# Gate and up products in two passes, the second with seven block products, and the sums of weight blocks on POOL

## Reference

```
x = x + linear_attention(q=layernorm(x), k=ctx, v=ctx)     # softmax of q over 16 dims, of k over tokens; 8 heads
h = layernorm(x)                                           # 2048 tokens x 1024
gate, up = h @ Wg.T, h @ Wu.T                              # Wg, Wu: 2752 x 1024 from codes and scales
x = x + (silu(gate) * up) @ Wd.T                           # Wd: 1024 x 2752
W = NF4[codes] * scales  (one scale per 64 inputs)
```

## Time and profile before

| what | value |
|---|---|
| median of 3 runs | 1540.36 us |
| profiled execution | 1539.45 us, its span 1537.7 us |
| PE busy | 1509.7 us, 98% |
| ACT busy | 921.8 us, 60% |
| DVE busy | 724.2 us, 47% |
| POOL busy | 60.9 us, 4% |
| DMA | 232.93 MB, mean 151 GB/s |

### The profile page before, as it was taken

The page is one execution under the profiler, slowest core; times in us unless marked ns, Lnnn a source line. Parts: engine busy times, 40 slices in busy tenths (PEclk is TensorE's granted clock), DMA queues, the critical chain, the costliest instruction groups (busy, mean ns, idle before and its releaser), DMA issues.

```text
span 1537.7 us, 18265 instructions
## 1 busy us (share of the span) xinstructions
PE 1509.7 (98%) x7056; PEld 1254.1 (82%) x7056; DVE 724.2 (47%) x1106; ACT 921.8 (60%) x1067; POOL 60.9 (4%) x99
## 2 busy tenths in 40 slices
PE   7999999999999999999999999999989999999998
PEld 6888788888888888888888888888768888888787
DVE  6998322322322222322322232222368888888764
ACT  6777876767677767676687767676223333333331
POOL 3343000000000000000000000000000000000000
PEclk9999999999999999999999999999999999999999
DMA  6554434444544454444443444436873535354332
GB/s 214 167 170 135 145 110 149 132 137 130 151 147 134 131 150 133 149 124 143 151 144 120 148 138 129 153 118 227 301 282 124 189 113 192 110 192 151 117 131 82
DMA packets 115462, 232.93 MB, mean 151 GB/s; under 512 B 8240, under 2 KB 55344, under 8 KB 110896
## 3 DMA queue, kind: packets, MB, share of 16 engines
q1 hardware_dynamic: 115376, 231.77, 46.9%
HBM read 154.14 MB, written 77.59 MB: 151 GB/s over the span
## 4 chain that ended last, share of the span: by engine, by line
PE 92%; ACT 4%; DMA 2%; issue 1%; DVE 1%; SPq 0%; DVEq 0%; POOL 0%; ACTq 0%
PE bank L1071 20%; PE bank L1069 20%; PE bank L1070 20%; PE bank L1116 8%; PE bank L1117 8%; PE bank L1118 8%; PE bank L1020 3%; PE bank L1047 1%; PE bank L1054 1%; DMA F<-inter_scratch 1%; PE bank L1037 1%; ACT early L602 1%; DMA inter_scratch<-F 1%; ACT F L615 1%; ACT F L636 1%
## 5 line engine op out<-in xcount | busy, mean ns | idle before, releaser
L1069 PE MATMUL bank<-R 128*128 128x512 f32 x1376 | 535.9, 389 | 0.0
L1070 PE MATMUL bank<-R 128*128 128x512 f32 x1376 | 535.7, 389 | 0.0
L1071 PE MATMUL bank<-R 128*128 128x512 f32 x1376 | 535.7, 389 | 0.0
L581 ACT ACTIVATE F<-F 128x1024 f32<-128x1024 f32 x441 | 467.6, 1060 | 13.3
L1070 PEld LDWEIGHTS bank<-R 128*128 128x128 f32 x1376 | 258.3, 188 | 53.7
L1071 PEld LDWEIGHTS bank<-R 128*128 128x128 f32 x1376 | 258.3, 188 | 53.6
L1069 PEld LDWEIGHTS bank<-R 128*128 128x128 f32 x1376 | 258.4, 188 | 53.3
L717 ACT COPY F<-bank 128x512 f32<-128x512 f32 x120 | 70.5, 587 | 271.0 <-PE bank L1118 267.1
L841 DVE TENSOR_TENSOR F<-F,bank 128x512 f32<-128x512 f32 x84 | 57.6, 686 | 331.1 <-issue 200.0
L648 ACT ACTIVATE F<-bank 128x512 f32<-128x512 f32 x84 | 49.8, 593 | 215.3 <-PE bank L1071 215.2
L767 DVE SCALAR_TENSOR_TENSOR F<-F 128x1024 f32<-128x1024 f32 x63 | 77.2, 1226 | 169.5 <-ACT F L581 169.5
(11 more groups left out here) (92 smaller groups left out, 1479.2 us busy)
## 6 DMA issues: line engine op xcount, KB each, us to landing
wf_scratch<-F SPq DMA_DIRECT2D x70, 512.0 KB, 3.5
inter_scratch<-F SPq DMA_DIRECT2D x84, 256.0 KB, 2.3
F<-in_gu_codes SPq DMA_DIRECT2D x41, 512.0 KB, 5.0
F<-in_gu_scales SPq DMA_DIRECT2D x82, 256.0 KB, 4.2
F<-inter_scratch SPq DMA_DIRECT2D x40, 512.0 KB, 3.8
R<-wf_scratch SPq DMA_DIRECT2D x20, 1024.0 KB, 5.9
FR<-wf_scratch SPq DMA_DIRECT2D x15, 1024.0 KB, 5.9
F<-in_d_codes SPq DMA_DIRECT2D x22, 512.0 KB, 4.4
```

The costliest lines, as they stand in the source:

```text
L581: nc.scalar.activation(y, y, ACT.Prelu, bias=bias, scale=scale, alpha=alpha).then_inc(bent, 1)
L1069: pe.matmul(dst, hi, xh[:, tb, t, :], start=(t == 0), stop=False)
L1070: pe.matmul(dst, hi, xl[:, tb, t, :], start=False, stop=False)
L1071: i = pe.matmul(dst, lo, xh[:, tb, t, :], start=False, stop=(t == HT - 1))
```

## The change

The gate and up stage is split into two passes over the chunks, counted by positions p. `FPOS` = 20 is the position of the half chunk and `FULL` = 21 that of chunk 20.

*Pass 1* does token blocks 0 and 1 as before, two blocks a position (44 entries in `BLOCKS`). In it each weight tile is made from its codes, stored to a new scratch tensor `w_scratch` (512 KB a tile), and split into high and low part by DVE alone (`split`: a copy and a subtraction). The tokens of blocks 2 and 3 are not split: their turned values stay in float32 (`xt`), and during the pass the seven sums and blocks of them are made, two a position, split, and (but for one) stored to `xf_scratch`. They come back as `xform`, each 2 MB.

*Pass 2* does token blocks 2 and 3 together. The matrix of a chunk is cut into gate and up rows and two halves of K, the tokens into two blocks and the same halves; seven products of 12 matmuls each replace eight. For the half chunk four products are enough. For each chunk one load of 1 MB brings gate and up weights back into `staged`, which is one buffer; POOL makes the four sums of its blocks; ACT copies the seven slices (high part) and DVE subtracts (low part). The tiles of Wd and their forms, one tile a position, are made in this pass only; formerly they were made over the whole stage. The buffers are laid out anew, the down stage's `wslot`, `stage`, `aform` and `yacc` with them, and its first loads are issued in another order.

The core of the diff (old lines first):

```diff
-            for c in range(FULL):
-                n = 2 + 3 * c
-                levels_of(act, n, n % 2, loads(n), None if c else last_turns)
-                silu_of(c, 0)
...
+            def weight_sums(p):
+                tt = nc.gpsimd.tensor_tensor
+                pool.wait_ge(staged_in, 16 * (p + 1))
+                wait(pool, wfl_ready, nth(p - 1, NP - 1) if p else 0)
+                wait(pool, ws_ready, p)
+                u = 2 * fulls(p)
+                tt(WS1, A21, A22, ALU.add).then_inc(ws_step, 1)
+                tt(WS3, A11, A21, ALU.subtract)
+                pool.wait_ge(ws_step, u + 1)
+                tt(WS2, WS1, A11, ALU.subtract).then_inc(ws_step, 1)
+                pool.wait_ge(ws_step, u + 2)
+                tt(WS4, A12, WS2, ALU.subtract).then_inc(ws_ready, 1)
+            for p in range(POS):
+                if p != FPOS:
+                    weight_sums(p)
...
...
+            def load_staged(p):
+                c = chunk_of(p)
+                if p:
+                    sp.wait_ge(wfl_ready, nth(p - 1, NP - 1))
...
+            for p in range(POS):
+                if p:
+                    store_pair_out(p - 1, 1)
+                next_item(WN + 2 + p)
+                if p == KW:
+                    store_rest(0)
+                    sp.wait_ge(form_stored, 16 * 2 * NP)
+                    load_w(0, 0)
+                if p + 1 < POS:
+                    load_staged(p + 1)
+                for tb in range(4):
+                    store_form(p, tb)
...
+                store_pair_out(p, 0)
# ACT, pass 1
+            for p in range(FPOS):
+                n = 2 * p + 2
+                if p:
+                    silu_block(2 * p - 1)
+                levels_of(act, n, 0, loads(n), None if p else last_turns)
+                xform_hi(2 * p - 2)
+                silu_block(2 * p)
+                levels_of(act, n + 1, 1, loads(n + 1))
+                xform_hi(2 * p - 1)
...
+            def wform_hi(p, i):
...
+                if p == 0:
+                    act.wait_ge(*((gate_done, 2 * FPOS + 3) if i < 4 else (up_done, ups_until(NB1 - 1))))
+                else:
+                    act.wait_ge(pair_done, nth(p - 1, i))
+                act.wait_ge(ws_ready, p + 1)
...
+                nc.scalar.copy(wslice[i][:, 0], src).then_inc(wfh_ready, 1)
# ACT, a full position of pass 2 (silu_x(p - 1) waits for the last product of p - 1)
+                    silu_x(p - 1)
+                for i in range(4, NP):
+                    wform_hi(p, i)
+                    bend_wd(p, 0, 1)
+                snap1(p)
+                form_hi(p, 0)
+                    bend_wd(p, 1, 2)
+                snapq(p)
+                form_hi(p, 1)
+                    bend_wd(p, 2, 3)
+                snap2(p)
+                bend_wd(p, 3, 4)
+                form_hi(p, 2)
+                wform_hi(p + 1, 0)
+                bend_wd(p, 4, 5)
+                silu_c(p)
+                wform_hi(p + 1, 1)
+                bend_wd(p, 5, 6)
+                wform_hi(p + 1, 2)
+                form_hi(p, 3)
+                bend_wd(p, 6, 7)
+                wform_hi(p + 1, 3)
+                bend_wd(p, 7, 8)
# DVE, a full position of pass 2
+                    pair_out(p - 1, 1)
+                for i in range(4, NP):
+                    wform_lo(p, i)
+                    weigh_wd(p)
+                    if p % 2:
+                        t_forms(p)
+                form_lo(p, 0)
+                form_lo(p, 1)
+                weight_sums(p + 1)          # two operations, for the half chunk only
+                form_lo(p, 2)
+                c11_sum(p)
+                wform_lo(p + 1, 0)
+                c22_sum(p)
+                wform_lo(p + 1, 1)
+                wform_lo(p + 1, 2)
+                form_lo(p, 3)
+                c21_sum(p)
+                pair_out(p, 0)
+                wform_lo(p + 1, 3)
# PE, a full position of pass 2 (before pair_product, each waits for wfl_ready of its slice)
+                pair_product(p, 0, X, True, True)
+                if p >= 2:
+                    pe.wait_ge(c21_ready, before)
+                pair_product(p, 1, Q, True, True)
+                pe.wait_ge(a1_ready, fulls(p) + 1)
+                pair_product(p, 2, X, False, True)
...
+                pair_product(p, 3, W, True, True)
+                pe.wait_ge(a2_ready, fulls(p) + 1)
+                pair_product(p, 4, X, False, True)
+                pe.wait_ge(aq_ready, fulls(p) + 1)
+                pair_product(p, 5, Q, False, True)
+                pe.wait_ge(c22_ready, fulls(p) + 1)
+                pair_product(p, 6, X, False, True)
```

More of the change, by code:

```diff
@@ new lines, in used, with nth, fulls @@
+        def used(p):
+            return (0, 1, 3, 6) if p == FPOS else tuple(range(NP))
+        def nth(p, i):
+            return sum(len(used(q)) for q in range(p)) + sum(j <= i for j in used(p))
+        def fulls(p):
+            return p if p <= FPOS else p - 1
+        wslice = [R2[:, i * N:(i + 1) * N].rearrange("p (q n) -> p q n", q=2) for i in range(NP)]
+        A11, A12, A21, A22 = [staged[:, i * WIDE:(i + 1) * WIDE] for i in range(4)]
+        WS1, WS2, WS3, WS4 = wsums
+        WFORMS = [A11, WS3, WS2, A12, WS1, A22, WS4]
@@ L220, in xattn_ffn @@
+        yacc = [early1[:, a:a + 2 * N].rearrange("p (t n) -> p t n", t=2) for a in y_at]
         AB, BK = 6 * P, 2 * P
[L221 to L225, removed]
@@ new lines, in xform_lo, with weight_sums @@
+            def xform_lo(k):
+                if not 0 <= k < XSTEPS:
+                    return
+                u, i, src, slot = xstep(k)
+                if i == 0:
+                    xform_sums(u)
+                dve.wait_ge(xph_ready, k + 1)
+                hi, lo = [xform[slot][:, q, u, :] for q in range(2)] if slot == DIRECT else form
+                if i < 3:
+                    hi, lo = wide(hi), wide(lo)
+                sub(lo, src, hi.bitcast(F32)).then_inc(xpl_ready, 1)
+            def weight_sums(p):
+                if p != FPOS:
+                    return
+                dve.wait_ge(staged_in, 16 * (p + 1))
+                nc.vector.scalar_tensor_tensor(WS3, A11, -2.0, A11, ALU.mult, ALU.add)
+                nc.vector.tensor_tensor(WS4, A11, A12, ALU.add).then_inc(ws_ready, 1)
@@ L1099, in _ @@
             pe.wait_ge(x1_ready, B)
[L1100 to L1108 removed]
+            gate(1)
+            up(1)
+            pe.wait_ge(xh_ready, B)
+            for k in range(2, NB1):
+                gate(k)
+                if BLOCKS[k][0] != FPOS:
+                    up(k)
@@ new lines, in pair_product @@
+            def pair_product(p, i, dst, start, stop):
+                wait(pe, wfl_ready, nth(p, i))
+                if p == 0:
+                    if i == DIRECT:
+                        pe.wait_ge(xpl_ready, XSTEPS)
+                    else:
+                        pe.wait_ge(xform_in[i], 16)
+                for j in range(HT // 2):
+                    hi, lo = [wslice[i][:, q, j * P:(j + 1) * P] for q in range(2)]
+                    a, b = start and j == 0, stop and j == HT // 2 - 1
+                    pe.matmul(dst, hi, xform[i][:, 0, j, :], start=a, stop=False, skip_group_check=not start)
+                    pe.matmul(dst, hi, xform[i][:, 1, j, :], start=False, stop=False, skip_group_check=not start)
+                    last = pe.matmul(dst, lo, xform[i][:, 0, j, :], start=False, stop=j == HT // 2 - 1, skip_group_check=not start)
+                last.then_inc(pair_done, 1)
```

702 lines of the change are left out of this document (488 added, 214 removed).

## The result

The changed kernel takes 1673.8 us (median of 4 runs, 1672.4 to 1677.6) against 1540.6 for the kernel before: the ratio is 1.0866, 95% interval 1.0846 to 1.0886. The forecast was slower, at 1604 us, with a range of 1560 to 1655. It is slower, but the measured time lies above the range.

What follows compares the result with a forecast made beforehand. The kernel before was taken as PE-bound, the changed pass 2 as bound by waits. -57.1 + 10 + 42.3 + 1.4 + 61.2 + 13.5 - 8 = +63.3 us on 1539.45 gave 1602.8, with 0.9 for the median 1604; range 1560 to 1655.

Steps and rivals of the forecast that it cites:

- Pass 1: First pass, costed at nothing: PE hides all other work at 21.8 us a position, ACT needing 19.4.
- The ring of pass 2: Second pass: a closed cycle of waits through ACT, SP, load and POOL, 23.7 us a position against PE's 19.0.
- the weights' ring: Pass 2, odd positions: staged load, POOL's sums, then ACT's slices; 23.7 us a position.
- the forms' ring: Pass 2, even positions: copy, low part and store through one form buffer before the next copy; 25.8 us.
- ACT's tail: End of a pass 2 position: ACT's slices, bends, silu and last form copy after POOL's sums, 6.92 us.
- One sign: Pass 2: ACT's copies of the slices wait for POOL by some 3 to 7 us in each position.
- the third: Pass 2, staged load of 1 MB: lands 5.9 us after issue, bounded by 3.8 and 6.6.
- The start of the down stage: PE's pauses of about 3 and 7 us there cost some 13; 5 were taken to remain: -8 us.
- That the forms do not queue: Rival for pass 2: even positions last as long as odd ones, 9 x 2.1 us less: 1585; chance 0.14.
- The clock: Rival for pass 2: PE's clock drops after two pauses a position, adding 30 us: 1634; chance 0.17.
- The ports: Rival for pass 2: POOL's sums are lengthened by DVE instructions on a shared port pair: 1618; chance 0.15.
- The faster case: Rival for pass 2: the ring is shorter than PE's 19.0 us, giving 1485; chance 0.12.

Runs made afterwards that it cites:

- the best version: All edits together (POOL making the sums), plus the last chunk's staged load first and the first form's store ahead of the scales: 1501.0 us, 0.9738 of the kernel before.
- single waits: The changed kernel, POOL still making the sums, with each slice's copy waiting only for what it reads: 1636.8 us.

## Why the prediction was right in its kind and wrong in its size

*Pass 1* was right: 443 matmuls in 100 us without idle time and with ACT at 87%. It began at 164.0 us and ended at about 633, and 2064 x 0.2267 is 468.

*The ring of pass 2* was right in place and order: the weights' ring closes odd positions, the forms' ring even ones. Of its terms, the issue of the load was 5.5 (5.45 forecast), the sums 5.54 (5.4), ACT's tail 6.93 (6.92). One sign did not come: ACT was to wait for POOL in every position, and did so 11 times only, in odd ones, the first and the half chunk; in even ones the wait for a form's store hides it.

*The step that failed* is the third, "I take 5.9, the median of the 1 MB loads". The load took 7.3 to 9.4 us, 8.5 in the median. Even my upper bound of 6.6 was too low. The rows that I took it from have other work in front: the 5.9 of the earlier trace rows has a plain read of 512 KB there, this one has two broadcast loads (each fills 64 partitions from one row of scales). With these cut small it was 5.6, with the load ahead of them 5.0. Odd positions lasted 26.4 us on average (23.7 forecast) and even ones 28.3 (25.8), since the form's store is behind the same load: 9 x 2.66 + 9 x 2.51 = 46.5 us. The first position took 33.9 instead of 29: its load left 3.9 us into it and needed 17.4 behind 4 MB, where I had counted 17 from the position's start. Position 19 took 19.7 instead of 20.4, and the last two took 46.9 instead of 43.4. Together pass 2 is 54 us over its sum.

*The start of the down stage* failed as well. I took 8 us off for loads that are done earlier, but the pauses grew from about 3 and 7 us to one of 22. The stage after the last product of the passes takes 1672.8 - 1225.6 = 447.2 us, against 1537.7 - 1101.0 = 436.7 before, 10.5 more where 8 less was forecast: 18.5 us. I had counted what the six loads of y save and not whom they stand in front of. In the trace the last block's store leaves behind them, and the stage's load that waits for it leaves 15 us later:

```profile
1230.31 2.29 SPq L494 DMA_DIRECT2D inter_scratch<-F  x1
1232.70 4.80 SPq L494 DMA_DIRECT2D inter_scratch<-F  x1
1237.55 4.72 SPq L551 DMA_DIRECT2D FR<-wf_scratch  x1
1247.69 0.36 SPq L560 DMA_DIRECT2D F<-inter_scratch  x1
```

Moving the loads of y took 5 us off the pauses and 1.8 off the stage. Why the stage stays 9 to 11 us longer than before in every kernel here is open beyond that: no run takes the rest of this chain apart. 54 + 18.5, less 0.7 of rounding and of the start, is the error of 71.8 against the profiled execution.

*The rivals.* That the forms do not queue was wrong: the first one's store was issued at 808.34, and ACT's copy could start at 816.67, 8.3 us later. The clock fell as that rival said, to 0.87 in the windows of pass 2, but added little there. The terms of the ring alone make up the whole of position 7, and ACT waited for PE's last product in six of the positions 0 to 18, for 3.4 us in all, where the rival had 30. The ports are in the trace, below. The faster case needed a ring of 19, and the best version has such a ring, but only with two form buffers, the load first, single waits and the first form's store ahead of the scales.

## What to carry to other kernels

When a kernel moves from full engines to a ring of waits, write down the ring with its single buffers, and price each DMA in it by what is in front of it in the same queue at that moment, not by its median. A wait on one ring is worth little alone while another ring is nearly as long: two form buffers gave 18 us and the order of the load 65, both together 119. Ask of each wait whether it names what the next instruction reads; here single waits took off as much (37 us) as moving the sums to the faster engine (32 us).

## What was not expected of the hardware

POOL's third sum took 1.71 or 1.72 us and not 1.26 where DVE made a form's low part, with two SBUF inputs, at the same time, and that one took 1.10 instead of 0.69. Lines of both in position 6:

```profile
816.61 1.26 POOL L735 TENSOR_TENSOR F<-F 128x512 f32<-128x512 f32 x1
817.32 1.10 DVE L1162 TENSOR_TENSOR F<-F 128x512 fp32r<-128x512 f32 x1 [10.24 <-ACT F L875]
817.83 1.72 POOL L737 TENSOR_TENSOR F<-F 128x512 f32<-128x512 f32 x1
```

Both fit an exclusive hold: DVE's end at 818.42 is 0.55 after the end of POOL's second sum, and POOL's third ends 1.13 after DVE's. This agrees with the rule of the Trainium skill (SBUF — State Buffer, "Who interferes with whom") that was weighed in the prediction; its price here is 0.46 us a position on POOL, where 0.69 was reckoned, and it is part of the 5.54. Where the two did not meet, with the staged load first, the sums took 5.05 to 5.16.

The broadcast loads of scales are dearer for their neighbours than for themselves: each of 256 KB lands in 4.1 us in the median, yet a load of 1 MB behind two of them takes 8.5 instead of 5.6. In the windows from 808 to 810 us, in position 6, with the load of 1 MB just issued behind them (807.71), the DMA engines are full (1.03 and 1.00) and move 299 and 234 GB/s. From 813, when the scales should have landed, they move 377; with plain loads in flight they moved 405 to 414. That it is the broadcast, and not the bytes, rests on the comparison with the 5.9 us behind 512 KB of a plain load; no run has the same bytes of scales without it.

```profile
808.00:809.00 1.00, 1.00 (x6) 0.81 (x6) 0.00 (x0) 0.00 (x0) 0.00 (x0) 1.00 1.03 299
809.00:810.00 1.00, 1.00 (x6) 0.84 (x5) 0.00 (x0) 0.00 (x0) 0.00 (x0) 1.00 1.00 234
813.00:814.00 1.00, 0.00 (x0) 0.00 (x0) 0.00 (x0) 0.00 (x0) 0.00 (x0) 1.00 0.97 377
```
